# Graph attention edge pass on one core: six buffers of gathered rows, three of the rest, and source lists kept on chip

## The chip, the cores and the metric

The kernel runs on one core of a Trainium2 chip. The metric is the device time of one execution in microseconds (us), lower is better. Engines are named as in the profile: PE is TensorE (PEld its weight loads), DVE is VectorE, ACT is ScalarE, POOL is GpSimd, SP is SyncE.

## What is computed

A graph layer followed by a mixture-of-experts layer. Cut to what the change touches:

```python
N_NODES = 6250                     # x is [6250, 256]; 200,000 edges, sorted by dst; 64 relations
Q = (enh @ Wq + bq).reshape(N, H, D)      # H = 4 heads, D = 64
K = (enh @ Wk + bk).reshape(N, H, D)
V = (enh @ Wv + bv).reshape(N, H, D)
src, dst = (edge_index[0], edge_index[1])
rel = rel_w[edge_relations]
mod_k = K[src] + 0.2 * rel[:, None, :]
scores = jnp.einsum('ehd,ehd->eh', Q[dst], mod_k) / D ** 0.5
seg_max = jax.ops.segment_max(scores, dst, num_segments=N)
ex = jnp.exp(scores - seg_max[dst])
denom = jax.ops.segment_sum(ex, dst, num_segments=N)
w = ex / denom[dst]
agg = jax.ops.segment_sum(w[:, :, None] * V[src], dst, num_segments=N)
```

Then an output projection, a layer norm, a router that picks two of eight experts for each node, the experts, and the combination of their outputs.

## The kernel before, in words

The program is a row of stages, each a block in which every engine has its own instruction stream, and no engine starts a stage before all have ended the last one. `prepare` (L444) makes a table of K and V rows in DRAM (`kv`, 516 float32 values per node), the transposed queries on chip (`QT`), and per-edge features in DRAM. `edge_pass` (L123) does all edges. Then come the node stage, the experts and the combination, which the change leaves alone.

**The edge pass** takes the sorted edges in 261 groups of 768 (`G = 6 * 128`). For one group the work is:

- SP (L186 to L197) loads the group's list of sources (`e_idx`, 128 x 6 integers, L189) and two broadcast rows of features (`e_rows`, L194, L196). Five steps behind, it stores the finished sums (`d_agg`, four DMAs, L207).
- POOL (L215 to L226) issues six gathers (L223), each of which fetches 128 rows of `kv` through one column of `e_idx`. Before them it waits until the sums of the group that last used the buffer are made (`s_agg`, L220) and until the list has landed (L221).
- PE (L354 to L429) turns the K half of the gathered rows (L363, 12 transposes, in two halves of six at two places of a step), multiplies one-hot features (L381) and keys (L386) into scores, adds the weighted V rows (L402, 48 small matmuls per group, which end the use of the gathered rows), and turns the probabilities (L427). A group comes to 12 + 4 + 8 + 2 + 48 + 2 + 4 + 6 = 86 matmuls and as many weight loads.
- DVE empties half of the turned keys (L302), makes `carry` (L312), the one-hot matrix (L317), the maximum (L323) and the sums (L335). ACT fills `e_qblock` from `QT` (L242, L246), empties the other half of the keys (L252), scales the carried sum (L263), takes the exponential (L270) and empties the turned probabilities (L282).

Step g of PE, DVE and ACT works on three groups at once: the key transposes of group g+1, the scores of group g, the sums of group g-1. So PE's step g-1 begins with the rows of group g, and the rows of group g are given back in the middle of step g+1. The order inside a step is written out by hand.

All buffers of the pass exist R = 4 times and the loop is unrolled by R. `pipeline` (L56) writes the first six steps and the last ones out, and puts four steps into the body of a hardware loop. With four buffers, the gathers of group g wait for the sums of group g-4:

```python
                    if g.first >= R:
                        pool.wait_ge(s_agg, g.t - (R - 1))
                    hold(pool, s_idx[g.slot], (g.rnd + 1) * 16)
```

In `prepare` POOL copies the source list from the input into `d_src` in DRAM (L575, L577). Edge e of a group stands at partition e // 6, column e % 6 there, and DVE writes the features of the edges in a matching order with strided reads (L644 to L647).

Of the kernel before, what the change touches and what calls it, by code (L numbers as in the profile page):

```python
# [25 lines left out]
NG = -(-E // G)  # L26
GH = G // 2
# [95 lines left out]
def edge_pass(nc, ctx, cst, QT, kv_dram, src_dram, featx_dram, feat_t_dram, agg_dram, bases, flag, penc, relT):  # L123
# [19 lines left out]
    carry = [sb(f"e_carry{i}", [P, P]) for i in range(R)]  # L143
    acc = [sb(f"e_acc{i}", [P, CW]) for i in range(R)]
    carried = [sb(f"e_carried{i}", [P, CW]) for i in range(R)]
    small = [sb(f"e_small{i}", [P, 8]) for i in range(R)]
# [9 lines left out]
    s_idx = [sem(f"es_idx{i}") for i in range(R)]  # L156
    s_rows = [sem(f"es_rows{i}") for i in range(R)]
    s_kv = [sem(f"es_kv{i}") for i in range(R)]
    s_out = [sem(f"es_out{i}") for i in range(R)]
# [18 lines left out]
    LO, HI, WARM = -1, 2, 6  # L178

    with nc.Block() as blk:  # L180
        @blk.sync
        def _(sp):
            def step(T):
                g = T(0)
                if g.live:

                    if g.first >= R:
                        hold(sp, s_kv[g.slot], g.rnd * (16 * TG))
                    sp.dma_start(idx[g.slot][:, :], src_dram[bass.ds(g.t, 1)].rearrange("a (p t) -> (a p) t", t=TG)  # L189
                                 ).then_inc(s_idx[g.slot], 16)  # L190

                    if g.first >= R:
                        hold(sp, s_oh, g.t - (R - 1))
                    sp.dma_start(rows[g.slot][0:NREL, :],  # L194
                                 feat_t_dram[bass.ds(g.t, 1)].to_broadcast([NREL, G])).then_inc(s_rows[g.slot], 16)
                    sp.dma_start(rows[g.slot][NREL:NR, :],  # L196
# [12 lines left out]
            pipeline(sp, NG, 0, 6, R, WARM, step)  # L209
            for i in range(R):  # L210
                sp.wait_ge(s_out[i], 16 * H * len(range(i, NG, R)))

        @blk.gpsimd
        def _(pool):
            def step(T):  # L215
                g = T(0)
                if g.live:

                    if g.first >= R:
                        pool.wait_ge(s_agg, g.t - (R - 1))  # L220
                    hold(pool, s_idx[g.slot], (g.rnd + 1) * 16)  # L221
# [5 lines left out]
            pipeline(pool, NG, 0, 0, R, WARM, step)  # L227

        @blk.scalar
        def _(act):  # L230
# [3 lines left out]
            def step(T):  # L234
                a = T(-1)
# [51 lines left out]
        def _(dve):  # L287
# [9 lines left out]
            def step(T):  # L297
# [6 lines left out]
                if a.live:  # L304
# [5 lines left out]
                    if a.first >= R:  # L310
                        dve.wait_ge(s_agg, a.t - (R - 1))
# [1358 lines left out]
```

## Time and profile before

| | us |
|---|---|
| Device time, median of 3 runs (4173.77 to 4175.83) | 4174.06 |
| Span of the profiled execution, first to last instruction | 3706.5 |
| What lies around that span, against the median | 467.6 |
| Stage `prepare` | about 0 to 196 |
| Edge pass | about 196 to 2446 |
| Node stage, experts, combination | about 2446 to 3706 |

The profile gives the span of the profiled execution, not its device time, so the third row is the median less the span. Over the span PE is busy 83%, DVE 42%, ACT 35%, POOL 50%, and DMA moves 192 GB/s. "Idle before" in a row is the time that the engine stood still just before those instructions, with what ended it; "issue" means that nothing the profile shows was waited for. A clock of 1.00 is TensorE's full 2.4 GHz, 0.50 is 1.2 GHz.

### The profile page before, as it was taken

The page shows a single profiled execution, that of the slowest core. Times are in us where ns is not written, and L with a number is a line of the kernel's source. Part 1 is how long each engine was busy: PE and PEld are TensorE (multiplying, and loading weights), DVE is VectorE, ACT ScalarE, POOL GpSimd, SP SyncE. Part 2 cuts the span into 40 slices and gives each one's busy share as a digit, 9 for nine tenths or more (in the row PEclk, how much of TensorE's full clock was granted, in tenths as well). Part 3 has the DMA queues.
Part 4 walks back from the last instruction along what each step waited for, and adds up shares of the span by engine and source line. Part 5 has one row for each costly group of instructions (what it writes and reads, how often), then busy time and mean ns, then how long its engine had stood idle before and what let it go on. Part 6 is the DMA issues. An engine that isn't in the chain of part 4 may idle for free. (4 is left out here: it accounts for less than half of the span.)

```text
span 3706.5 us, 94365 instructions
## 1 busy us (share of the span) xinstructions
PE 3077.7 (83%) x27466; PEld 2203.1 (59%) x27466; DVE 1568.6 (42%) x4831; ACT 1314.4 (35%) x3767; POOL 1844.9 (50%) x1996
## 2 busy tenths in 40 slices
PE   6968888888888888888888888867749999999940
PEld 3645555555555555555555555544538888888840
DVE  7734444444444444444444444469941111111123
ACT  1234444444444444444444444423322222222210
POOL 3256777766666666766676666636640000000036
PEclk9978999998899998988899898875559999999975
DMA  7567777777777777776787677744445555555534
GB/s 239 174 185 203 219 222 222 222 211 202 202 209 208 209 204 202 221 200 192 197 222 203 194 214 201 204 126 141 146 162 177 193 175 192 173 195 176 192 101 143
DMA packets 420214, 710.74 MB, mean 192 GB/s; under 512 B 132319, under 2 KB 289783, under 8 KB 420006
## 3 DMA queue, kind: packets, MB, share of 16 engines
q0 software_dynamic: 137328, 450.71, 42.4%
q1 hardware_dynamic: 282822, 259.35, 22.3%
q14 instruction: 46, 0.38, 0.0%
q8 instruction: 18, 0.29, 0.0%
HBM read 637.81 MB, written 72.79 MB: 192 GB/s over the span
## 5 line engine op out<-in xcount | busy, mean ns | idle before, releaser
L223 POOL DMA_INDIRECT e_kv<-d_kv,e_idx x1566 | 1507.7, 963 | 733.7 <-issue 469.8
L363 PE MATMUL psK<-consts,e_kv 128*128 128x128 f32 x3132 | 487.6, 296 | 308.7 <-DMA e_kv<-d_kv,e_idx 308.3
L363 PEld LDWEIGHTS psK<-consts,e_kv 128*128 128x128 f32 x3132 | 363.4, 149 | 379.9 <-issue 345.9
L1577 POOL DMA_INDIRECT c_y<-d_ys,c_idx x98 | 96.4, 984 | 854.6 <-DVE c_idx L1553 825.0
L386 PE MATMUL psD<-e_kT,e_qblock 128*64 128x384 f32 x2088 | 519.4, 581 | 0.0
L302 DVE COPY e_kT<-psK 128x384 f32<-128x384 f32 x522 | 288.5, 553 | 494.3 <-PE psK L363 479.6
L323 DVE TENSOR_REDUCE e_small<-psD 128x1 f32<-128x768 f32 x261 | 249.9, 957 | 512.0 <-PE psD L386 512.0
L1429 ACT ACTIVATE f_hT<-f_psH,f_b 128x256 f32<-128x256 f32 x448 | 212.1, 473 | 590.4 <-PE f_psH L1503 590.4
L263 ACT ACTIVATE e_carried<-psA,e_small 128x65 f32<-128x65 f32 x261 | 82.6, 317 | 922.4 <-PE psA L402 922.4
L1503 PE MATMUL f_psH<-f_xT,f_w 128*128 128x256 f32 x1792 | 398.3, 381 | 1.4 <-DMA f_w<-in_W 1.4
L1493 PE MATMUL f_psY<-f_w,f_hT 128*128 128x256 f32 x1792 | 396.1, 379 | 0.0
L1503 PEld LDWEIGHTS f_psH<-f_xT,f_w 128*128 128x128 f32 x1792 | 342.2, 191 | 48.5 <-DMA f_w<-in_W 1.7
L1493 PEld LDWEIGHTS f_psY<-f_w,f_hT 128*128 128x128 f32 x1792 | 336.3, 190 | 43.3
L252 ACT COPY e_kT<-psK 128x384 f32<-128x384 f32 x522 | 247.8, 475 | 211.6 <-PE psK L363 207.0
L282 ACT COPY e_probT<-psP 128x512 f32<-128x512 f32 (+1 forms) x522 | 224.5, 482 | 71.0 <-PE psP L427 70.4
L381 PE MATMUL psD<-e_onehot,e_qrel_high 98*128 98x384 f32 x522 | 248.3, 476 | 0.0
L402 PE MATMUL psA<-e_kv,e_probT 128*32 128x65 f32 x12528 | 241.9, 228 | 0.3 <-ACT e_probT L282 0.3
L427 PE MATMUL psP<-consts,e_prob 128*128 128x128 f32 x1566 | 228.4, 282 | 12.0 <-ACT e_prob L270 1.9
L270 ACT ACTIVATE e_prob<-psD,e_small 128x768 f32<-128x768 f32 x261 | 234.2, 897 | 5.3 <-DVE e_small L329 5.3
L381 PEld LDWEIGHTS psD<-e_onehot,e_qrel_high 98*128 98x128 f32 x522 | 109.7, 210 | 193.5 <-issue 193.4
L1449 DVE TENSOR_SCALAR f_xT<-f_psT,f_ln 128x256 f32<-128x256 f32 x112 | 55.7, 539 | 398.5 <-PE f_psT L1481 398.5
L402 PEld LDWEIGHTS psA<-e_kv,e_probT 128*32 128x32 f32 x12528 | 198.2, 113 | 19.0 <-ACT e_probT L282 0.5
(202 smaller groups left out, 3766.8 us busy)
## 6 DMA issues: line engine op xcount, KB each, us to landing
f_w<-in_W SPq DMA_DIRECT2D x112, 1024.0 KB, 7.3
e_rows<-d_featt SPq DMA_DIRECT2D x261, 96.0 KB
e_kv<-d_kv,e_idx POOLq DMA_INDIRECT x1566
d_agg<-e_acc SPq DMA_DIRECT2D x1044, 8.1 KB
f_xs<-d_xs SPq DMA_DIRECT2D x56, 256.0 KB, 2.6
d_ys<-f_y SPq DMA_DIRECT2D x56, 256.0 KB, 2.2
e_rows<-d_featx SPq DMA_DIRECT2D x261, 51.0 KB
d_kv<-p_kv SPq DMA_DIRECT2D x48, 258.0 KB, 2.5
```

The lines of the kernel that those rows point to most:

```text
L223: pool.indirect_dma_start(out=kv[g.slot][:, t, :], out_offset=None, in_=kv_dram[:, :], in_offset=bass.IndirectOffsetOnAxis(ap=idx[g.slot][ ...
L252: act.copy(kT[a.slot % 2][:, 1, j * GH:(j + 1) * GH], psK[:, 1, 0:GH]).then_inc(s_kTa, 1)
L270: act.activation(prob[g.slot][:, :].rearrange("p (c q) -> p c q", c=2), psD[:, :, 0:GH], ACT.Exp, bias=small[g.slot][:, NM], scale=SCALE). ...
L302: dve.tensor_copy(kT[a.slot % 2][:, 0, j * GH:(j + 1) * GH], psK[:, 0, 0:GH]).then_inc(s_kTv, 1)
L323: dve.tensor_reduce(sm[:, MX], psD[:, :, 0:GH], AX.XY, ALU.max).then_inc(s_m, 1)
L363: mm = pe.transpose(psK[:, half, t * P:(t + 1) * P], kv[a.slot][:, third * 3 + t, half * P:(half + 1) * P], ident)
L381: pe.matmul(psD[:, c, 0:GH], part[0:NR, :], onehot[g.slot][0:NR, cols], start=k == 0, stop=False)
L386: mm = pe.matmul(psD[half, c, 0:GH], qblock[g.slot][:, b, half], kT[g.slot % 2][:, b, cols], start=False, stop=True, tile_position=(0, hal ...
L402: mm = pe.matmul(psA[h * W:(h + 1) * W, 0:CW], probT[c.slot][:, t, h * W:(h + 1) * W], kv[c.slot][:, t, D + h * CW:D + (h + 1) * CW], star ...
L427: mm = pe.transpose(psP[:, j, (t - lo) * P:(t - lo + 1) * P], prob[g.slot][:, t * P:(t + 1) * P], ident)
L1493: mm = pe.matmul(psY[:, t, 0:D], hT[:, f, t * P:(t + 1) * P], w2[c.slot][:, f, :], start=f == 0, stop=f == FC - 1)
L1503: mm = pe.matmul(psH[:, f % 4, 0:BT], w1[g.slot][:, a, f * P:(f + 1) * P], xT[g.slot][:, a, :], start=a == 0, stop=a == DC - 1)
```

## The change

In the edge pass the unrolling and the buffers of `idx`, `kv`, `carry`, `acc`, `carried` and `small` go from 4 to U = 6, and all others (`rows`, `onehot`, `qblock`, `qrel`, `prob`, `probT`) from 4 to R = 3. The body of the hardware loop holds six steps instead of four, and eight steps stand ahead of it instead of six. The list of sources of a group no longer comes by a DMA from DRAM. All lists stand on chip in `idxall`, and ACT copies six columns of it, five steps ahead of its other work. The gathers of group g wait for the sums of group g-6.

In `prepare` the copy to `d_src` goes. POOL clears a part of `ends` and loads the input's list into it in three DMAs, 128 sources a row. After its other work of the stage, DVE converts the list to float32, PE turns it in 13 transposes of 128 x 128, and DVE writes them back as integers. Edge e of a group now stands at partition e % 128, column e // 128, so the features are written in their own order with plain reads.

```diff
+IT = -(-E // (P * P))
-def edge_pass(nc, ctx, cst, QT, kv_dram, src_dram, featx_dram, ...
+def edge_pass(nc, ctx, cst, QT, kv_dram, idxall, featx_dram, ...
-    R = 4
+    U = 6
+    R = 3
-    idx = [sb(f"e_idx{i}", [P, TG], I32) for i in range(R)]
+    idx = [sb(f"e_idx{i}", [P, TG], I32) for i in range(U)]
-    kv = [sb(f"e_kv{i}", [P, TG, KVW]) for i in range(R)]
+    kv = [sb(f"e_kv{i}", [P, TG, KVW]) for i in range(U)]
...
-    LO, HI, WARM = -1, 2, 6
+    LO, HI, WARM = -1, 2, 8
+    AHEAD = U - 1
...
                     if g.first >= R:
-                        hold(sp, s_kv[g.slot], g.rnd * (16 * TG))
-                    sp.dma_start(idx[g.slot][:, :], src_dram[bass.ds(g.t, 1)].rearrange("a (p t) -> (a p) t", t=TG)
-                                 ).then_inc(s_idx[g.slot], 16)
-
-                    if g.first >= R:
                         hold(sp, s_oh, g.t - (R - 1))
...
-                    if g.first >= R:
-                        pool.wait_ge(s_agg, g.t - (R - 1))
-                    hold(pool, s_idx[g.slot], (g.rnd + 1) * 16)
+                    if g.first >= U:
+                        pool.wait_ge(s_agg, g.t - (U - 1))
+                    hold(pool, s_idx, g.t + 1)
...
             def step(T):
+                n = T(-AHEAD)
+                if n.live:
+
+                    if n.first >= U:
+                        act.wait_ge(s_kv[n.slot], n.rnd * (16 * TG))
+                    act.copy(idx[n.slot][:, :], idxall[:, bass.ds(n.t * TG, TG)]).then_inc(s_idx, 1)
                 a = T(-1)
...
-            pipeline(act, NG, LO, HI, R, WARM, step)
+            pipeline(act, NG, -AHEAD, HI, U, WARM, step)
```

In `prepare`:

```diff
-            pool.dma_start(dram["src"].rearrange("g e -> (g e)")[0:E].rearrange("(a b) -> a b", b=1250),
-                           io["src"].rearrange("(a b) -> a b", b=1250)).then_inc(s_z, 16)
-            pool.dma_start(dram["src"].rearrange("g e -> (g e)")[E:NSRC].rearrange("(a b) -> a b", a=1),
-                           zero[0:1, 0:NSRC - E].bitcast(I32)).then_inc(s_z, 16)
+            pool.memset(ends[:, IT - 1, :], 0).then_inc(s_zero, 1)
+            pool.wait_ge(s_zero, 4)
+            pool.dma_start(ends[:, 0:IT - 1, :], io["src"][0:(IT - 1) * P * P].rearrange("(c r p) -> r c p", p=P, r=P)
+                           ).then_inc(s_src, 16)
...
-                link(dve.tensor_scalar(feat[c][0][0:n, :].rearrange("g (t p) -> g t p", t=TG),
-                                       epos2[0:n, :].rearrange("g (p t) -> g t p", t=TG), -1.0, None, ALU.max))
-                link(dve.tensor_copy(feat[c][1][0:n, :].rearrange("g (t p) -> g t p", t=TG),
-                                     edge[c][1][0:n, :].rearrange("g (p t) -> g t p", t=TG)))
+                link(dve.tensor_scalar(feat[c][0][0:n, :], epos2[0:n, :], -1.0, None, ALU.max))
+                link(dve.tensor_copy(feat[c][1][0:n, :], edge[c][1][0:n, :]))
...
+            dve.wait_ge(s_src, 48)
+            dve.tensor_copy(endsf[:, :, :], ends[:, :, :]).then_inc(s_back, 1)
+            for i, c in enumerate(range(0, IT, 4)):
+                n = min(IT - c, 4)
+                dve.wait_ge(s_turn, i + 1)
+                dve.tensor_copy(idxall[:, c * P:(c + n) * P], psI[:, i % 2, 0:n * P]).then_inc(s_back, 1)
...
+            pe.wait_ge(s_back, 1)
+            for i, c in enumerate(range(0, IT, 4)):
+                if i >= 2:
+                    pe.wait_ge(s_back, i)
+                for j in range(min(IT - c, 4)):
+                    mm = pe.transpose(psI[:, i % 2, j * P:(j + 1) * P], endsf[:, c + j, :], ident)
+                mm.then_inc(s_turn, 1)
```

## Rows read from the trace of the kernel before

**Rows 1.** Waits of the whole span: engine, line, releaser: us in total, times, longest.

```profile
ACT e_carried L263 <- PE psA L402: 922.4, 261, 6.2
...
PE psK L363 <- DMA e_kv<-d_kv,e_idx: 308.3, 187, 21.0
POOL e_kv L223 <- PE psA L402: 246.5, 108, 4.8
```

**Rows 2.** The gathers' line: times, duration ns min/median/max, first and last start.

```profile
L223 POOL DMA_INDIRECT e_kv<-d_kv,e_idx x1566: 940/946/1353, 199.1 to 2422.1; - x196
```

**Rows 3.** Groups by line: busy us, mean ns | idle before and its releasers.

```profile
L223 POOL DMA_INDIRECT e_kv<-d_kv,e_idx x1566 | 1507.7, 963 | 733.7 <-issue 469.8 <-PE psA L402 246.5 <-DMA e_idx<-d_src 17.3
```

**Rows 4.** Timeline of the first groups: start, duration, instruction, [idle before <-releaser].

```profile
206.69 0.95 POOL L223 DMA_INDIRECT e_kv<-d_kv,e_idx  x1 [0.30 <-issue]
207.94 0.95 POOL L223 DMA_INDIRECT e_kv<-d_kv,e_idx  x1 [0.30 <-issue]
...
227.03 0.82 PE L363 MATMUL psK<-consts,e_kv 128*128 128x128 f32 x6
...
233.67 0.82 PE L363 MATMUL psK<-consts,e_kv 128*128 128x128 f32 x6
```

**Rows 5.** Timeline of the regular stretch, one round of the buffers' chain.

```profile
433.96 0.89 PE L402 MATMUL psA<-e_kv,e_probT 128*32 128x65 f32 x48
...
434.98 0.32 ACT L263 ACTIVATE e_carried<-psA,e_small 128x65 f32<-128x65 f32 x1 [3.29 <-PE psA L402]
...
435.74 0.95 POOL L223 DMA_INDIRECT e_kv<-d_kv,e_idx  x1 [0.79 <-issue]
...
438.29 0.87 PE L363 MATMUL psK<-consts,e_kv 128*128 128x128 f32 x6 [1.12 <-DMA e_kv<-d_kv,e_idx]
...
441.94 0.89 PE L402 MATMUL psA<-e_kv,e_probT 128*32 128x65 f32 x48
441.99 0.94 POOL L223 DMA_INDIRECT e_kv<-d_kv,e_idx  x1 [0.30 <-issue]
...
446.04 0.87 PE L363 MATMUL psK<-consts,e_kv 128*128 128x128 f32 x6 [0.90 <-DMA e_kv<-d_kv,e_idx]
```

**Rows 6.** Timeline of the irregular stretches: a late gather, and a step at half clock.

```profile
2408.37 0.94 POOL L223 DMA_INDIRECT e_kv<-d_kv,e_idx  x1 [2.13 <-PE psA L402]
```

```profile
783.35 1.46 PE L363 MATMUL psK<-consts,e_kv 128*128 128x128 f32 x6 [1.63 <-DMA e_kv<-d_kv,e_idx]
...
791.60 0.82 PE L363 MATMUL psK<-consts,e_kv 128*128 128x128 f32 x6
```

**Rows 7.** Windows: us, PE, PEld, DVE, ACT, POOL busy (count), clock, DMA share, GB/s.

```profile
400.00:600.00 200.00, 172.32 (x2151) 114.50 (x2150) 96.47 (x275) 92.19 (x275) 146.34 (x151) 1.00 0.79 221
...
1000.00:1500.00 500.00, 433.07 (x4992) 285.72 (x4993) 225.98 (x638) 216.14 (x642) 335.38 (x350) 0.91 0.74 206
```

```profile
2115.00:2140.00 25.00, 20.84 (x262) 13.96 (x260) 11.93 (x35) 11.38 (x34) 17.85 (x19) 1.00 0.82 233
```

**Rows 8.** Timeline: a gather that starts inside DVE's one-hot instruction.

```profile
447.28 0.61 DVE L317 TENSOR_SCALAR e_onehot<-e_rows,consts 98x768 fp32r<-98x768 bf16 x1
447.41 1.30 POOL L223 DMA_INDIRECT e_kv<-d_kv,e_idx  x1 [0.30 <-issue]
```

**Rows 9.** Timeline of DVE at the start of the program.

```profile
13.95 0.89 DVE L644 TENSOR_SCALAR p_place<-p_epos 128x768 bf16<-128x768 f32 x1
...
15.74 0.56 DVE L637 CAST p_epos<-p_dst 128x768 f32<-128x768 int32 x1
...
42.58 0.43 DVE L674 BATCH_NORM_STATS2 p_stat<-p_x 128x6 f32<-128x256 f32 x1 [3.01 <-DMA p_x<-in_x]
```

**Rows 10.** Timeline of the change from `prepare` to the edge pass.

```profile
188.68 0.41 DVE L707 TENSOR_TENSOR p_q<-p_psQ,p_bias 128x256 f32<-128x256 f32 x1
...
189.16 0.25 SPq L544 DMA_DIRECT2D d_kv<-p_kv  x1
...
196.67 0.27 DVE L289 MEMSET e_qblock<- 128x256 f32 x1 [7.58 <-PEq L513]
...
199.60 0.22 ACT L242 COPY e_qblock<-QT 64x32 f32 x1 [1.77 <-DVE e_prob L294]
```

**Rows 11.** Timeline of DVE in the node stage, just after its loop's branch back.

```profile
2629.09 0.42 DVE L1163 TENSOR_TENSOR n_y<-n_psO,n_xn 128x256 f32<-128x256 f32 x1 [3.17 <-issue]
```

**Rows 12.** Windows of one round each: DVE's node loop, and the edge loop.

```profile
2629.00:2668.00 39.00, 27.09 (x88) 18.54 (x88) 34.81 (x160) 12.08 (x42) 26.60 (x35) 0.59 0.46 145
430.30:464.60 34.30, 30.21 (x360) 19.94 (x362) 16.78 (x47) 15.60 (x47) 25.07 (x26) 1.00 0.80 221
```

More of the change, by code:

```diff
@@ L142, in edge_pass @@
     probT = [sb(f"e_probT{i}", [P, TG, P]) for i in range(R)]
[L143 to L146, printed above, removed]
+    carry = [sb(f"e_carry{i}", [P, P]) for i in range(U)]
+    acc = [sb(f"e_acc{i}", [P, CW]) for i in range(U)]
+    carried = [sb(f"e_carried{i}", [P, CW]) for i in range(U)]
+    small = [sb(f"e_small{i}", [P, 8]) for i in range(U)]
     kT = [sb(f"e_kT{i}", [P, DC, G]) for i in range(2)]
@@ L155, in edge_pass @@
     ident = cst("ident")
[L156 to L159, printed above, removed]
+    s_idx = sem("es_idx")
+    s_rows = [sem(f"es_rows{i}") for i in range(U)]
+    s_kv = [sem(f"es_kv{i}") for i in range(U)]
+    s_out = [sem(f"es_out{i}") for i in range(U)]
     s_init = sem("es_init")
@@ L208, in step @@
                                      ).then_inc(s_out[o.slot], 16)
-            pipeline(sp, NG, 0, 6, R, WARM, step)
-            for i in range(R):
-                sp.wait_ge(s_out[i], 16 * H * len(range(i, NG, R)))
+            pipeline(sp, NG, 0, 6, U, WARM, step)
+            for i in range(U):
+                sp.wait_ge(s_out[i], 16 * H * len(range(i, NG, U)))
         @blk.gpsimd
@@ L291, in _ @@
                 dve.tensor_scalar(qrel[i][1][:, :], cst("pen"), 0.0, None, ALU.mult)
-            dve.memset(acc[R - 1][:, :], 0.0).then_inc(s_init, 1)
-            dve.memset(small[R - 1][:, :], 0.0).then_inc(s_init, 1)
+            dve.memset(acc[U - 1][:, :], 0.0).then_inc(s_init, 1)
+            dve.memset(small[U - 1][:, :], 0.0).then_inc(s_init, 1)
             dve.memset(prob[0][:, 0:1], 0.0).then_inc(s_init, 1)
@@ L316, in step @@
                         dve.wait_ge(s_d, a.t - (R - 1))
-                    dve.tensor_scalar(onehot[a.slot][0:NR, :], rows[a.slot][0:NR, :], cst("match")[0:NR, :], None,
+                    dve.tensor_scalar(onehot[a.slot % R][0:NR, :], rows[a.slot % R][0:NR, :], cst("match")[0:NR, :], None,
                                       ALU.is_equal).then_inc(s_oh, 1)
@@ L379, in step @@
                         cols = slice(c * GH, (c + 1) * GH)
-                        for k, part in enumerate(qrel[g.slot]):
-                            pe.matmul(psD[:, c, 0:GH], part[0:NR, :], onehot[g.slot][0:NR, cols],
+                        for k, part in enumerate(qrel[g.slot % R]):
+                            pe.matmul(psD[:, c, 0:GH], part[0:NR, :], onehot[g.slot % R][0:NR, cols],
                                       start=k == 0, stop=False)
@@ L413, in step @@
                     pe.wait_ge(s_carry, a.t + 1)
-                    pe.matmul(psX[:, 0:1], carry[a.slot][:, :], small[(a.slot - 1) % R][:, MM], start=True, stop=True)
+                    pe.matmul(psX[:, 0:1], carry[a.slot][:, :], small[(a.slot - 1) % U][:, MM], start=True, stop=True)
                     pe.wait_ge(s_qb, a.t * 2 + 2)
                     for b in range(DC):
-                        mm = pe.matmul(psX[0:NREL, P:2 * P], relT, qblock[a.slot][:, b, :],
+                        mm = pe.matmul(psX[0:NREL, P:2 * P], relT, qblock[a.slot % R][:, b, :],
                                        start=b == 0, stop=b == DC - 1)
@@ L480, in prepare @@
     place = sb("p_place", [P, G])
+    ends = sb("p_ends", [P, IT, P], I32)
+    endsf = sb("p_endsf", [P, IT, P])
     misfit = sb("p_misfit", [P, 4])
```

58 lines of the change are left out of this document (34 added, 24 removed).

## The prediction

> **What bounds the kernel now.** I read the waits first. They name a ring of two: PE waits 308.3 us for gathered rows, and POOL, which issues the gathers, waits 246.5 us for PE's sums, that is, for a free buffer [rows 1]. Neither engine is full, so I read the gathers' line next. They run from 199.1 to 2422.1 us, with the last one's 0.95 us 2224.0 us for 261 groups, 8.52 us a group [rows 2]. They are busy 1507.7 us of that; 246.5 us is the wait for PE and the rest is issue time [rows 3]. Three periods then decide the case.
>
> POOL alone: where nothing holds it, a gather starts 1.25 us after the one before, 0.95 us of work and 0.30 us between two [rows 4]. The median of 946 ns makes that gap 0.304 us, and the mean of 963 ns makes a mean pitch of 1.267 us [rows 2, 3]. Six of them are 7.60 us a group.
>
> PE alone: at full clock and with its rows there, one step follows the other in 233.67 - 227.03 = 6.64 us [rows 4].
>
> The ring: from the end of the sums at 434.85 to the first gather 0.89 us; that gather to the sixth's end at 442.93, 7.19 us; until PE starts on the rows at 446.04, 3.11 us; and from a step's start at 438.29 to the end of its sums at 442.83, 4.54 us [rows 5]. That is 15.73 us. With four buffers it spans two steps (the rows of group g are needed at step g-1, and the buffer comes free in step g-3), so a step takes at least 7.87 us. The regular stretch shows 8.0 (2151 matmuls at 86 a group are 25.0 groups in 200 us), at clock 1.00. The middle shows 8.61 (4992 matmuls, 58.0 groups in 500 us), at 0.91 [rows 7]. There the ring has no slack: a wait of 1.63 us for rows came with a clock of 0.50, that step took 8.25 us instead of 6.64, its sums came late, and a later gather waited, as the one of 2.13 us did [rows 6].
>
> **The change, part by part.**
>
> *Six buffers of gathered rows.* The ring now spans four steps: 15.73 / 4 = 3.93 us a step. It stops binding, and POOL's own 7.60 us is the largest period left. All 1566 gathers then take 1566 x 1.267 = 1984.1 us, against 2224.0: minus 239.9 us. POOL no longer waits for PE unless PE falls behind by about two groups, 15 us. What is late next is the gather's issue itself: PE will wait 7.60 - 6.64 = 0.96 us a step, less than the 1.12 us that went with clock 1.00 [rows 5, 7]. Should the clock fall at times, a step of 8.25 us [rows 6] among steps of 6.64 still averages under 7.60, and the filled buffers carry it.
>
> *How sure is 1.267?* The part above 946 ns comes from DVE: a gather that began 0.13 us into the one-hot instruction took 1.30 us [rows 8]. How often they meet depends on the phase, which the change moves. None meeting gives 6 x 1.25 = 7.50 us; the worst, one of 1353 ns [rows 2] in each group, gives 7.91. So the gathers take 1957 to 2065 us, the change gives minus 267 to minus 159 us. I take the mean of today, since the phase today wanders over both.
>
> *The list copied by ACT.* It costs one small copy a group, nearest to the 0.22 us of a `qblock` copy [rows 10], and a few register instructions: 0.2 to 0.5 us. It stands ahead of the `qblock` copies, the key copy, and then the wait for the sums; ACT is idle 3.29 us a step at that wait, 922.4 us in all [rows 1, 5]. In a step of 6.64 us the idle time would still be near 2. Cost nothing; without that cover 0.5 x 261 = 130 us. Its wait for rows of group g-1 has long been met when ACT has finished that group's step. POOL needs the list some four groups later, 30 us. A late list would bring back what was removed.
>
> *The list's DMA and SP.* One DMA fewer and one hold fewer a group on SP, and 128 small pieces less for the DMA engines. No one waited for either but once, 17.3 us at the start, where it stood for the whole change of stage [rows 3]. Gain between nothing and a little less load; I take nothing.
>
> *Three buffers for the rest.* `prob`, `probT`, `onehot`, `qrel` and `qblock` of group g-3 are finished before the step in which group g overwrites them; the waits are met by the order of the steps. `rows` of a group is loaded when the one-hot of three groups before is made and after SP has stored the sums of its step, so some two steps, 15 us, before DVE wants it, one step less than now. Nothing, unless that load took 15 us.
>
> *The loop of six steps.* Priced among the rivals.
>
> *The turned lists in `prepare`.* DVE's conversion: 1664 columns at the 0.56 us for 768 [rows 9] are 1.2 us. 13 transposes at half clock, six in 1.46 [rows 6], are 3.2 us. The copies back, at DVE's 0.41 us for 256 columns out of PSUM [rows 10], are 0.82 us for 512, 2.7 us in all for three and a short one. In series 7.1 us, overlapped about 5.5. DVE ended its work at 189.1 and stood still 7.58 us, because the last store of `kv`, issued at 189.16, had not landed [rows 10]. The work fits into that: nothing, at worst 2 us. On POOL the new memset and one more DMA are a microsecond before a wait of many. DVE's plain reads save up to 0.89 - 0.56 = 0.33 us in each of six instructions, 2 us at most, but 8 us later DVE waits 3.01 us for a DMA [rows 9]; I take nothing.
>
> *Start.* POOL's first gather waits for ACT's first copy instead of a DMA. ACT is free when DVE's clearing ends, which loses one buffer of four, and its first work stood at 199.60 behind a load of a register [rows 10]. Within half a microsecond of now.
>
> **Sum.** 4174.06 - 239.9 = 3934.2, and I forecast 3934. The durations come from the profiled execution, whose span is 3706.5 us; its own device time is not given, so I take what lies around the span (467.6 us) as unchanged and start from the median. The measurement can tell about 0.2%, 8 us, from no change.
>
> **The rivals.**
>
> *The transfers don't keep up.* At 7.60 us a group the DMA engines must deliver 221 x 8.0 / 7.60 = 233 GB/s. Against: one window did 233 at a share of 0.82 [rows 7], and the first gathers ran at full pitch. For: no long stretch has shown more than 221. Held at 8.0 us a group, the gathers take 2088 us: 4038.
>
> *The loop no longer stays where instructions are kept; this one ends slower.* In the node stage DVE stands still 3.17 us after its branch back, for nothing the profile shows, in a round of 160 of its instructions [rows 11, 12]. In the edge pass PE ran some 360 matmuls and as many weight loads a round, and no such wait shows [rows 12]; with six steps it is some 1,030. If it no longer stays, PE stands still in each of 42 rounds, and each such wait costs the clock too: 3.17 + 1.61 = 4.8 us. PE has 6 x 0.96 = 5.8 us of slack a round, so one wait is hidden. The forecast's gain is 5.7 us a round, so beyond 11.5 us, at three waits (14.3), the kernel is slower: 42 x (14.3 - 5.8) = 357, 4291. Against: PE's larger rounds have shown no wait where DVE's small one has, so PE has more room.
>
> The Trainium skill (Runtime: NRT & Kernel Launch, Instruction fetch mechanics) gives the store as 32 KiB for most engines and 128 KiB, 2048 instructions, for PE, and says that a taken branch whose target lies outside the current window of two pages of 256 instructions forces a fetch. By the first figure six steps fit and the forecast stands; by the second even the body of before would have stalled each round, and rows 12 speak against that for PE.
>
> *The edit does not do what it says.* A list that comes late, or one of the three-fold buffers that binds, keeps the ring at about its old length: 4174, no change.
>
> **How the numbers follow.** Forecast, POOL's issue binds: 0.80, with its own range of 3907 to 4015. Transfers hold it at 8.0: 0.11. No change: 0.04. Slower by the loop: 0.05. The last three and the ends make up two in ten outside 3900 to 4018. Faster 0.91, same 0.04, slower 0.05.
>
> **What would show it.** Right: the gathers' idle time before them nearly all issue, the wait for `psA` L402 gone; first to last gather 1984 us apart; PE waiting for rows at nearly each of 261 steps, about 1 us each; clock near 1.00 in the pass; windows near 230 GB/s. The step on DVE is right if gathers still average 963 ns. Wrong: POOL waiting for sums or for ACT's copy; PE or DVE idle by issue every sixth group; gathers landing ever later behind their issue.

## The result, and the profile after

| | before, us | after, us |
|---|---|---|
| Median on record | 4174.89 (4173.77 to 4175.83, 4 runs) | 4198.30 (4192.23 to 4201.73, 4 runs) |
| Ratio, 95% interval | | 1.0051 (1.0037 to 1.0065) |
| Span of the profiled execution | 3706.5 | 4194.8 |
| Its device time | not given | 4196.65 |
| Edge pass, first to last work of an engine | 2245.2 | 2713.8 |

The forecast was 3934 in a range of 3900 to 4018; the changed kernel is 0.5% slower than the one before. The third and fourth lines hold the key. Around the span of the changed kernel lie 1.9 us, not 467.6. So the page of before describes an execution of some 3708 us, by this account, and the executions of 4174 us were others, of which no profile was shown.

The experiments show that there are two conditions, which I name by what the kernel **before** takes in the same comparison. In the light one it takes 3676 to 3742 us and the changed kernel 3471: the medians lie 237.5 us apart, and the 95% interval of the ratio makes that 215 to 251, so the forecast gain of 240 us is there. In the heavy one it takes 4174 to 4185 and the changed kernel 4198. The comparison on record is of the heavy kind.

First the waits of the changed kernel on record (engine, line, what was waited for: us in total, times, longest):

```profile
ACT e_kT L256 <- remote: 960.6, 249, 26.1
POOL e_kv L221 <- PE psA L406: 777.2, 255, 16.5
DVE e_small L327 <- remote: 631.6, 229, 17.0
PEld psA L406 <- issue: 489.3, 521, 2.3
PE psA L406 <- issue: 420.4, 485, 2.2
POOL e_kv L221 <- issue: 399.0, 1310, 0.3
```

PE's wait for gathered rows, 308.3 us before [rows 1], is gone (17.1 us in 4194.8, all of it at the start of the pass). That part of the change works. But POOL's wait for PE's sums did not go away, it trebled, from 246.5 us [rows 1] to 777.2. So PE is late, not POOL. And PE stands still 420.4 us inside its own run of 48 small matmuls, for "issue": nothing that the profile shows. Before, no such row stood among the large ones. ACT and DVE wait for "remote", a signal whose sender the trace doesn't name.

The gathers themselves are as fast as ever, and nobody waits for them (the gathers' line: duration min/median/max, first and last start; then what their engine waited for, and who waited for them):

```profile
L221 POOL DMA_INDIRECT e_kv<-d_kv,e_idx x1566: 940/946/1359, 199.0 to 2875.1; - x196
  PE psA L406: 777.2, 255
  issue: 399.0, 1310
  ACT e_idx L238: 17.9, 1
  PE psK L367: 21.8, 2
```

They take 946 ns as before [rows 2], but their last start is at 2875.1 instead of 2422.1. In the middle PE starts on a group's rows 26 us after the group's last gather was issued.

The windows of the pass (window, its length, busy us and count of PE, PEld, DVE, ACT and POOL, clock, DMA share, GB/s):

```profile
400.00:600.00 200.00, 164.77 (x1695) 111.79 (x1696) 75.27 (x216) 76.17 (x233) 110.89 (x117) 0.88 0.64 172
1000.00:1500.00 500.00, 416.04 (x4160) 288.62 (x4158) 186.20 (x531) 188.28 (x582) 279.87 (x292) 0.86 0.63 172
```

A group has 86 matmuls, so 4160 of them are 48.4 groups in 500 us: 10.34 us a group. The same window of before held 4992, 8.61 us a group [rows 7]. Every period below comes from this window in this way, unless it is called a mean. The clock is lower, 0.86 instead of 0.91, and so is the data rate, 172 GB/s instead of 206 to 221. PE does not wait for rows, so nothing here points at the transfers.

What a stall looks like, in order of time (start, length, engine, line, operation, tile, count, and in brackets the idle time before it):

```profile
1012.12 0.87 PE L390 MATMUL psD<-e_kT,e_qblock 128*64 128x384 f32 x4
...
1013.28 0.43 PE L406 MATMUL psA<-e_kv,e_probT 128*32 128x65 f32 x15
1013.69 0.52 SPq L192 DMA_DIRECT2D e_rows<-d_featt  x1
1014.12 0.95 POOL L221 DMA_INDIRECT e_kv<-d_kv,e_idx  x1 [0.30 <-issue]
1015.19 0.72 SPq L194 DMA_DIRECT2D e_rows<-d_featx  x1
1015.21 0.22 PE L406 MATMUL psA<-e_kv,e_probT 128*32 128x65 f32 x1 [1.50 <-issue]
1016.64 0.74 PE L406 MATMUL psA<-e_kv,e_probT 128*32 128x65 f32 x32 [1.21 <-issue]
1016.67 0.48 ACT L256 COPY e_kT<-psK 128x384 f32<-128x384 f32 x1 [4.39 <-remote]
1016.81 0.96 DVE L327 TENSOR_REDUCE e_small<-psD 128x1 f32<-128x768 f32 x1 [3.34 <-remote]
```

PE does 15 small matmuls in 0.43 us, stands still 1.50 us, does one, stands still 1.21 us, and then does the other 32 in 0.74. ACT and DVE, which had been free for 4.39 and 3.34 us, go on at 1016.67 and 1016.81, in the very moment in which PE does. DVE's instruction reads `psD`, whose last matmul had ended at 1012.99, so the signal reached DVE late. POOL goes on issuing meanwhile, at its 0.95 us and 0.30 between.

### The profile page after: what moved, and what is told of

The parts are those of the page before. It is cut to its first block and busy times, and to the rows that moved or that the text cites. A ratio compares the mean times of both kernels' runs of the same rounds, so it can differ in the third digit from the quotient of the medians.

```text
span 4194.8 us, 93348 instructions
## 1 busy us (share of the span) xinstructions
PE 3383.0 (81%) x27479; PEld 2460.7 (59%) x27479; DVE 1560.9 (37%) x4833; ACT 1363.5 (33%) x4028; POOL 1837.5 (44%) x1998
## 5 line engine op out<-in xcount | busy, mean ns | idle before, releaser
L221 POOL DMA_INDIRECT e_kv<-d_kv,e_idx x1566 | 1500.8, 958 | 1194.1 <-PE psA L406 777.2
L406 PE MATMUL psA<-e_kv,e_probT 128*32 128x65 f32 x12528 | 374.0, 227 | 423.4 <-issue 420.4
L406 PEld LDWEIGHTS psA<-e_kv,e_probT 128*32 128x32 f32 x12528 | 260.6, 110 | 510.6 <-issue 489.3
L367 PE MATMUL psK<-consts,e_kv 128*128 128x128 f32 x3132 | 526.1, 313 | 31.9 <-DMA e_kv<-d_kv,e_idx 17.1
L390 PE MATMUL psD<-e_kT,e_qblock 128*64 128x384 f32 x2088 | 472.2, 532 | 0.0
L367 PEld LDWEIGHTS psK<-consts,e_kv 128*128 128x128 f32 x3132 | 424.3, 163 | 59.6 <-issue 36.3
L431 PE MATMUL psP<-consts,e_prob 128*128 128x128 f32 x1566 | 320.9, 361 | 20.5 <-issue 10.6
L431 PEld LDWEIGHTS psP<-consts,e_prob 128*128 128x128 f32 x1566 | 239.8, 185 | 96.8 <-issue 54.5
L421 PE MATMUL psX<-e_qblock,relT 128*64 128x128 f32 x1044 | 242.0, 374 | 0.0
L385 PE MATMUL psD<-e_onehot,e_qrel_high 98*128 98x384 f32 x522 | 237.1, 454 | 5.7 <-DVE e_qrel_high L345 5.7
```

The costliest lines, as they stand in the source:

```text
L221: pool.indirect_dma_start(out=kv[g.slot][:, t, :], out_offset=None, in_=kv_dram[:, :], in_offset=bass.IndirectOffsetOnAxis(ap=idx[g.slot][ ...
L367: mm = pe.transpose(psK[:, half, t * P:(t + 1) * P], kv[a.slot][:, third * 3 + t, half * P:(half + 1) * P], ident)
L385: pe.matmul(psD[:, c, 0:GH], part[0:NR, :], onehot[g.slot % R][0:NR, cols], start=k == 0, stop=False)
L390: mm = pe.matmul(psD[half, c, 0:GH], qblock[g.slot % R][:, b, half], kT[g.slot % 2][:, b, cols], start=False, stop=True, tile_position=(0, ...
L406: mm = pe.matmul(psA[h * W:(h + 1) * W, 0:CW], probT[c.slot % R][:, t, h * W:(h + 1) * W], kv[c.slot][:, t, D + h * CW:D + (h + 1) * CW], ...
L421: mm = pe.matmul(psX[0:NREL, P:2 * P], relT, qblock[a.slot % R][:, b, :], start=b == 0, stop=b == DC - 1)
```

## The experiments

### Does the light condition exist on its own, and what does each half of the change do there?

Kernel before, sent as it is:

> The kernel before itself, unchanged, to see the execution behind its usual time of 4174 us. Theory A (PE is held to about 10.3 us a group by something that fills up, in both kernels): span about 4172, a group every 10.3 us, freezes of 1 to 2 us inside the 48 small matmuls of line 402, POOL waiting for psA for some 750 us. Theory B (the page of before shows its usual execution, and 467 us lie around the span): span about 3706, a group every 8.5 us, freezes absent, and the slower steps of the changed kernel come from the change.

The lists on chip with four buffers, the changed kernel with

```diff
-    U = 6
-    R = 3
+    U = 4
+    R = 4
-    LO, HI, WARM = -1, 2, 8
+    LO, HI, WARM = -1, 2, 6
```

> The changed kernel with four buffers of everything and a loop of four steps, so only the source lists on chip remain of the change. Theory A: PE's period is the same 10.3 us a group as before and after, time within 0.5% of 4174; whatever makes the changed kernel 0.5% slower shows as a difference either to this or to before. Theory B: about the time of before, with the step of 8.5 us back, if the six-step loop or the six buffers brought the freezes; 4198 with a step of 10.3 us if ACT's list copy brought them.

Measured on one chip: before 3724.02 us (3695.05 to 3779.25, 10 runs), against 3726.25 for the runs of before beside it, ratio 1.0018 (0.9971 to 1.0064); lists alone 3614.30 (3611.14 to 3622.67), ratio 0.9702 (0.9630 to 0.9774). Theory A, which had the stalls in every execution, fell: the edge pass takes 2230.1 us and no small matmul stands still. So did the other half of Theory B, the 467 us around the span: the profiled execution took 3695.05 us with a span of 3693.2. Then the changed kernel itself on another chip, and the six buffers without the lists, that is the kernel before with

```diff
-    R = 4
+    U = 6
+    R = 3
-    kv = [sb(f"e_kv{i}", [P, TG, KVW]) for i in range(R)]
+    kv = [sb(f"e_kv{i}", [P, TG, KVW]) for i in range(U)]
...
-    LO, HI, WARM = -1, 2, 6
+    LO, HI, WARM = -1, 2, 8
```

> The changed kernel once more, unchanged, beside the kernel before on one chip, since before ran in 3726 us in the last runs and its own two-buffer ring shows there with no freezes. Theory C (the 10.3 us a group of the recorded result belongs to the chip or the moment, where before would take 4174 too; elsewhere POOL's issue binds as forecast): about 3726 - 240 = 3486 us, a group every 7.6 us, POOL hardly waiting for psA. Theory D (the changed kernel itself brings the freezes, on any chip): about 4198 us and a group every 10.3 us, whatever before takes.

> Six buffers of gathered rows, three of the rest and the loop of six steps, but the source lists still loaded from DRAM by SP and the preparation as before. Theory C: nearly all of the gain is here, within 15 us of the changed kernel, about 3490 us. Theory D with its cause in the loop or the buffers: about 4198 us here as well; with its cause in ACT's list copy (the lists-only kernel took 3614, so it would need both): about 3490 us.

Measured: the changed kernel 3471.11 us (3468.75 to 3472.67, 4 runs), ratio 0.9372 (0.9324 to 0.9420); six buffers alone 3471.38 (3470.24 to 3473.48), ratio 0.9376 (0.9328 to 0.9424); before beside them 3708.64. Theory C held: one and the same program takes 4198 us in the one condition and 3471 in the other. So with six buffers the lists are worth nothing (0.3 us), and the buffers, with the loop of six steps that comes with them, do all of it. The two were not taken apart in the light condition.

The middle window, 1000 to 1500, of before again, of the lists alone and of the changed kernel in the light condition:

```profile
1000.00:1500.00 500.00, 433.82 (x4988) 287.17 (x4987) 224.73 (x639) 215.55 (x638) 333.89 (x349) 0.91 0.75 206
```

```profile
1000.00:1500.00 500.00, 431.30 (x5246) 286.31 (x5246) 235.50 (x671) 230.43 (x733) 357.32 (x367) 0.97 0.78 216
```

```profile
1000.00:1500.00 500.00, 454.51 (x5666) 303.72 (x5664) 255.48 (x724) 250.07 (x786) 379.98 (x395) 0.99 0.82 232
```

8.62, 8.20 and 7.59 us a group; the clock rises from 0.91 to 0.99. And the waits of the changed kernel in the light condition:

```profile
ACT e_carried L267 <- PE psA L406: 798.1, 261, 5.6
POOL e_kv L221 <- issue: 452.1, 1484, 0.3
PEld psK L367 <- issue: 218.6, 197, 17.4
PE psK L367 <- DMA e_kv<-d_kv,e_idx: 177.0, 173, 17.2
```

This is the picture that the forecast drew: POOL is held by its own issue (its wait for sums is 24.7 us), and it is PE that waits for rows, though at 173 of the 261 steps and not at nearly each.

### In the heavy condition: is it POOL, the ring, or PE's small matmuls?

Three changes of the changed kernel, which met the heavy condition (before 4175.90 us, 4175.53 to 4180.07, 7 runs). The sixth gather replaced by a plain DMA of 128 rows on SP:

```diff
+                    if g.first >= U:
+                        hold(sp, s_agg, g.t - (U - 1))
+                    sp.dma_start(kv[g.slot][:, TG - 1, :], kv_dram[0:P, :]).then_inc(s_kx[g.slot], 16)
...
-                    for t in range(TG):
+                    for t in range(TG - 1):
```

> The changed kernel, but the sixth gather of each group is replaced by a plain DMA of 128 rows of the same table on SP (so the values of a sixth of the edges are other rows than the reference's; bytes and rows moved stay the same). Theory I (the issue of the gathers on POOL bounds the changed kernel, at six times 1.26 us = 7.57 us a group): five issues take 6.3 us, PE's own step of 6.64 us is then the longest, the period falls to 6.65 to 6.9 us and the time on a chip where the kernel before takes 3709 falls from 3471 to 3471 - 0.93 x 261 = 3228, up to 3295. Rival II (the transfers bound it, at 233 GB/s): as many bytes in as many rows are moved, so the period stays at 7.57 and the time at 3471. Where the kernel before takes 4174 on this chip: the period stays near 10.3 whatever POOL does, 4198.

The ring shortened to four steps again, all else kept:

```diff
-                        pool.wait_ge(s_agg, g.t - (U - 1))
+                        pool.wait_ge(s_agg, g.t - (U - 3))
```

> The changed kernel with six buffers, six steps in the loop and the lists on chip, but the gathers of group g wait for the sums of group g-4, as with four buffers. Theory I (the ring is what the change removed): the period goes back to 8.1 us, as in the kernel that had the lists alone (8.14, 3614 us), on a chip where the kernel before takes 3709 to 3726. Rival (the larger loop, or the three-fold buffers, is what made it faster, or the unroll matters by itself): it stays at 7.57 and 3471. Where the kernel before takes 4174: 10.3 us a group and 4198 either way, since the ring had long been loose there (buffers filled 25 us early).

Half of the small matmuls left out:

```diff
-                        for t in range(lo, hi):
+                        for t in range(lo, hi, 2):
                             for h in range(H):
                                 mm = pe.matmul(psA[h * W:(h + 1) * W, 0:CW], ...
```

> The changed kernel with only half of the 48 small matmuls of the sums (L406; the odd sixths of a group are left out of the sums, so the output lacks them). Where the kernel before takes 3709 to 3726: Theory I (POOL's issue bounds, PE has 0.93 us a step to spare) says no change, 3471 within 10 us; were PE the bound, 24 x 0.03 to 0.05 us a step less, 3471 - 0.7 to 1.3 x 261 = 3130 to 3290. Where the kernel before takes 4174: if the limit there is the rate at which PE's dense runs of small matmuls and weight loads may go, some 48 of 187 PE instructions a group fewer give 10.3 x 139/187 = 7.6 to 9.0 us a group, 3490 to 3860; if the limit lies outside PE, the period stays near 10.3 and the time near 4198.

Measured: five gathers 3824.99 us (3815.13 to 3825.81), ratio 0.9150 (0.9135 to 0.9166); ring of four 4199.17 (4196.72 to 4203.48), ratio 1.0055; half the sums 4100.84 (4099.96 to 4104.10), ratio 0.9820 (0.9804 to 0.9836). The ring is indeed without effect here, but the kernel with it did not meet the light condition, in which it would have told the buffers from the loop. Halving the small matmuls takes 97 us or 0.37 us a group. PE needs 0.89 us for 48 of them [rows 5], 0.44 for the 24 left out, so the relief is no more than their own work, and their density is where the stalls show and not what they come from. The surprise is the first: my expectation for this condition was "near 10.3 whatever POOL does", and taking one gather of six from POOL, at as many bytes and rows moved, takes 373 us or 1.43 us a group. PE's stalls fall by half with it, and the granted clock goes back to nearly full (the kernel with five gathers, waits and middle window):

```profile
PEld psA L411 <- issue: 236.1, 312, 1.4
PE psA L411 <- issue: 192.0, 275, 1.4
```

```profile
1000.00:1500.00 500.00, 418.75 (x4856) 275.16 (x4857) 211.23 (x620) 224.61 (x682) 268.02 (x284) 0.99 0.71 200
```

The clock is the larger part of this. The windows of the whole pass, of the changed kernel in the heavy condition, of the one with five gathers, and of the changed kernel in the light condition:

```profile
200.00:2910.00 2710.00, 2225.91 (x22446) 1521.31 (x22446) 1006.22 (x2871) 1016.34 (x3123) 1499.83 (x1566) 0.87 0.63 170
```

```profile
200.00:2540.00 2340.00, 1942.37 (x22418) 1280.56 (x22422) 982.59 (x2870) 1029.96 (x3131) 1237.54 (x1305) 0.98 0.71 197
```

```profile
200.00:2200.00 2000.00, 1811.50 (x22391) 1208.63 (x22392) 1016.16 (x2870) 992.00 (x3120) 1504.20 (x1566) 0.98 0.82 231
```

The granted clock has two levels here, 1.00 and 0.50. It stood at 0.50 for 696 us of the changed kernel's pass, in 664 of which PE was busy, and for 88 and 68 us with five gathers. Six transposes take 1.46 us at half clock and 0.82 at full [rows 6]. If all of PE's work shrinks like these, an estimate, the low clock costs 664 x (1 - 0.82 / 1.46) = 291 us or 1.11 us a group in the one and 0.11 in the other. So of the 1.43 us some 1.0 is the clock that came back, and some 0.4 is the gather that was taken away.

### No gathers, half the rows, half the bytes

So I asked what the gathers do to the other engines. No gather in the pass at all, SP fetching 768 rows by one DMA:

```diff
-                    for t in range(TG):
-                        pool.indirect_dma_start(
...
+                    sp.dma_start(kv[g.slot][:, :, :], kv_dram[0:G, :].rearrange("(t p) d -> p t d", t=TG)
+                                 ).then_inc(s_kv[g.slot], 16)
```

> The changed kernel without any gather in the edge pass: SP fetches 768 fixed rows of the same table for each group with one plain DMA of as many bytes in as many rows (so the sums are of other rows than the reference's). Theory S (on a chip where the kernel before takes 4174, what holds PE, SP and ACT up and makes 10.3 us of a group is the gathers that POOL issues): nothing is held up, no stall inside PE's 48 small matmuls, and PE's own step of 6.64 to 6.9 us bounds the pass, 196 + 261 x 6.7 + 1260 = 3210, up to 3290, on either kind of chip. Rival (it is the transfers' rows and bytes, or the density of PE's instructions, whoever issues them): on such a chip the stalls stay, the group takes 9 us or more and the kernel 3830 or more. On a chip where the kernel before takes 3709 both say 3210 to 3290, unless 1.58 MB in 6.64 us (238 GB/s beside the rest) is more than the transfers manage; then 3471.

Gathers of 64 rows, and gathers of 128 rows of half the length (the buffers are cleared once at the start in both, which costs some 20 us):

```diff
-                            out=kv[g.slot][:, t, :], out_offset=None, in_=kv_dram[:, :],
-                            in_offset=bass.IndirectOffsetOnAxis(ap=idx[g.slot][:, t:t + 1], axis=0),
+                            out=kv[g.slot][0:P // 2, t, :], out_offset=None, in_=kv_dram[:, :],
+                            in_offset=bass.IndirectOffsetOnAxis(ap=idx[g.slot][0:P // 2, t:t + 1], axis=0),
```

```diff
-                            out=kv[g.slot][:, t, :], out_offset=None, in_=kv_dram[:, :],
+                            out=kv[g.slot][:, t, 0:KVW // 2], out_offset=None, in_=kv_dram.rearrange("n (a b) -> (n a) b", a=2),
```

> The changed kernel with gathers of 64 rows instead of 128 (as many instructions on POOL, half the rows and half the bytes; the other half of the edges gets zeros). Where the kernel before takes 4174: Theory S1 (the stalls go with the number of rows gathered): from five gathers of 128 in place of six, 1.43 us a group for 128 rows; 384 fewer rows bring the group down to PE's own step, 6.7 to 7.5 us, 3210 to 3420. Theory S2 (they go with the number of gather instructions): 10.3 us a group, 4198. Where the kernel before takes 3709: if POOL's 0.95 us a gather goes with its rows, PE's step of 6.64 bounds, 3230; if it is a fixed price, the group stays at 7.57 us and the kernel at 3471.

> The changed kernel with gathers of 128 rows of half the length (1032 bytes instead of 2064: as many instructions and rows, half the bytes; the rest of each row is zeros, so the output is another). Where the kernel before takes 4174: Theory S1 (rows) and S2 (instructions) say 10.3 us a group and 4198; Theory S3 (bytes moved for gathers) says as much relief as with half the rows, 3210 to 3420. Where the kernel before takes 3709: Theory I (the issue bounds, not the bytes) says 7.5 us a group, 3450 to 3471; were it the bytes, PE's step bounds, 3230.

These three met the light condition (before 3741.92 us; one of its seven runs took 14353.51 us at full clock, and nothing here explains it): no gathers 3217.30 (3215.30 to 3219.97), ratio 0.8615 (0.8567 to 0.8664); 64 rows 3410.29 (3404.89 to 3415.52), ratio 0.9135; half the length 3498.02 (3490.36 to 3501.79), ratio 0.9370. The middle windows of the three, in this order:

```profile
1000.00:1500.00 500.00, 500.00 (x6500) 346.00 (x6504) 291.34 (x826) 289.14 (x900) 0.00 (x0) 1.00 0.82 266
```

```profile
1000.00:1500.00 500.00, 471.32 (x5887) 314.88 (x5876) 266.50 (x757) 261.89 (x827) 374.71 (x412) 1.00 0.52 134
```

```profile
1000.00:1500.00 500.00, 452.95 (x5676) 301.79 (x5673) 261.72 (x726) 251.03 (x789) 379.37 (x397) 1.00 0.51 129
```

Without gathers PE is busy all the time, at 6.62 us a group, and 266 GB/s flow. With half the bytes in as many rows the group takes 7.58 us, as with all the bytes (7.59): bytes don't bound it. With half the rows a gather takes 0.91 us instead of 0.96, so nearly all of it is a fixed price of the instruction, and the group takes 7.30.

The first two were run again until both had met the heavy condition.

> The same kernel as e7 (no gathers on POOL, one plain DMA of 768 rows a group on SP), which took 3217 us where the kernel before takes 3742, sent again in the hope of a chip on which the kernel before takes 4174. There: Theory S (what holds the engines up is the gathers that POOL issues) says 6.65 us a group and 3210 to 3230, no stall in the small matmuls and no slow register instruction on SP; the rival (rows and bytes whoever issues them, or PE's dense runs) says 9 us or more a group, 3830 or more. On a chip of the other kind: 3217 again, which tells nothing new.

> The same kernel as e8 (gathers of 64 rows instead of 128), which took 3410 us where the kernel before takes 3742. On a chip where the kernel before takes 4174: S1 (the hold-up goes with the rows gathered) says the group falls from 10.3 us to 7.3 (POOL's issue of 64 rows, as measured) up to 8.2, 3410 to 3650; S2 (it goes with the number of gather instructions) says 10.3 us a group, 4198. On a chip of the other kind: 3410 again.

> The kernel without gathers on POOL once more, for a chip on which the kernel before takes 4174. There Theory S (the gathers that POOL issues cause the hold-ups) says 3210 to 3230 and no stall in the small matmuls; the rival (rows and bytes whoever issues them, or PE's dense runs) says 3830 or more. On a chip of the other kind: 3217 again.

> The kernel with gathers of 64 rows once more. On a chip where the kernel before takes 4174: S1 (the hold-up goes with the rows gathered) says 3410 to 3650; S2 (with the number of gather instructions) says 4198. On a chip of the other kind: 3412 again.

> The kernel without gathers on POOL once more, for a chip on which the kernel before takes 4174. There Theory S (the gathers that POOL issues cause the hold-ups) says 3210 to 3230 and no stall in the small matmuls; the rival (rows and bytes whoever issues them, or PE's dense runs) says 3830 or more. On a chip of the other kind: 3217 again.

> The kernel with gathers of 64 rows (384 rows a group in six instructions), sent again now that without gathers the kernel took 3239 where the kernel before takes 4182. On such a chip: S1 (the hold-up goes with the rows gathered) says the group falls from 10.3 us to 7.3 up to 8.2, 3410 to 3650; S2 (with the number of gather instructions) says 10.3 us a group, 4198. On a chip of the other kind: 3412 again.

> The kernel with gathers of 128 rows of half the length (1032 bytes). On a chip where the kernel before takes 4174 to 4182: S1 and S2 (rows or instructions) say 10.3 us a group and 4198 to 4220; S3 (the bytes that gathers move) says 7.6 to 8.8 us a group, 3500 to 3800. On a chip of the other kind: 3498 again.

> The kernel with gathers of 64 rows, one last time. On a chip where the kernel before takes 4174 to 4182: S1 (the hold-up goes with the rows gathered) says 3410 to 3650; S2 (with the number of gather instructions) says 4198 or more. On a chip of the other kind: 3410 to 3417 again.

| run | before, us | this, us | ratio (95%) |
|---|---|---|---|
| no gathers, second | 3725.01 | 3215.97 | 0.8673 (0.8627 to 0.8720) |
| 64 rows, second | 3725.01 | 3413.53 | 0.9206 (0.9157 to 0.9254) |
| no gathers, third | 3734.44 | 3218.33 | 0.8621 (0.8534 to 0.8708) |
| 64 rows, third | 3734.44 | 3416.33 | 0.9151 (0.9058 to 0.9244) |
| **no gathers, fourth** | **4182.15** | **3239.01** | 0.7745 (0.7722 to 0.7767) |
| 64 rows, fourth | 3676.36 | 3417.49 | 0.9293 (0.9266 to 0.9320) |
| half the length, second | 3676.36 | 3502.81 | 0.9525 (0.9498 to 0.9553) |
| **64 rows, fifth** | **4185.27** | **4262.87** | 1.0184 (1.0154 to 1.0214) |

The two bold lines decide. Without gathers the kernel takes nearly the same in both conditions, and its window in the heavy one is that of the light one:

```profile
1000.00:1500.00 500.00, 500.00 (x6460) 345.44 (x6458) 290.73 (x826) 289.56 (x901) 0.00 (x0) 1.00 0.81 266
```

Its edge pass takes 1753.9 us there and 1753.2 in the light condition. As many bytes and rows moved by SP, and 48 small matmuls as dense as ever, and no stall: Theory S is shown as it was put, the rival (rows and bytes, or PE's density) fell. SP fetches the same 768 neighbouring rows for every group, however, and through another queue. So whether it is the instruction on POOL, the queue that its packets go through or the scattered rows that holds PE up, this run alone can't tell. Half the rows in as many gathers, on the other hand, bring no relief at all, which speaks against the scattered rows. The waits and the middle window of that kernel in the heavy condition:

```profile
POOL e_kv L224 <- PE psA L412: 881.4, 255, 17.4
PEld psA L412 <- issue: 516.3, 525, 2.2
PE psA L412 <- issue: 446.8, 510, 2.7
```

```profile
1000.00:1500.00 500.00, 415.17 (x4116) 290.60 (x4115) 184.49 (x523) 185.50 (x573) 261.81 (x287) 0.84 0.36 94
```

10.45 us a group at 94 GB/s, against 7.30 us of the same kernel in the light one. S2 held: the stalls (446.8 us instead of 420.4) go with the number of gather instructions, not with their rows. Rows of half the length met the light condition both times, so for those nothing is known of the heavy one. All of these kernels but the ring of four compute other sums, so none is a remedy; one instruction that gathers more rows, which would lower their number, was not tried.

## Why the prediction was wrong

**The step that failed** is in the sum: "its own device time is not given, so I take what lies around the span (467.6 us) as unchanged and start from the median". Nothing of that size lies around a span: 1.9 us do in the changed kernel. The 467.6 us lay inside executions in another condition. Of them 1.9 us belong around the span. If before loses as much in the node stage and the combination as the changed kernel does (3.3 and 14.6 us, last section), 448 us are left for the pass, 1.72 us a group on top of 8.52 [rows 2]: 10.24. The changed kernel's gathers, counted in the same way, take (2875.1 + 0.95 - 199.0) / 261 = 10.26 us a group. (No profile of before in the heavy condition was taken; this is worked out.) So there the longest period was already PE's step with what the gathers cost it, and not the ring that the forecast loosens. In the changed kernel the ring of four is hidden below it (ring of four 4199, ring of six 4198), and loosening it could win nothing. What makes the changed kernel 0.5% slower was not found; it is not the longer ring. The three rivals of the prediction all reasoned from the same page and so missed it too. The one without a change came near in its time, 4174, by luck, for its reason was another: neither did a list come late nor did a buffer of the three-fold ones bind.

The remaining terms can be held against the light condition, for which the page of before is a true picture:

- *The gain.* 3708.64 - 3471.11 = 237.5 us (215 to 251 by the interval), forecast 239.9. The gathers start from 199.0 to 2180.1 us, with the last one's 0.95 us 1982 us, forecast 1984.1.
- *POOL's period.* Mean over the groups from the eighth on 7.60 us, forecast 7.60; a gather's mean is 0.961 us instead of 0.963, so DVE's share stayed as I took it.
- *PE's step.* 6.62 to 6.66 us without gathers, forecast 6.64.
- *The ring.* With the lists alone the mean is 8.17 us, my bound was 7.87; a ring of six has its buffer free 14 us before POOL wants it (median).
- *Transfers as the rival.* Fell: 232 GB/s are held for the whole pass, and 266 without gathers.
- *The larger loop as the rival.* Fell: no stall comes every sixth group in the light condition, and the six-step loop gives 3471 with the lists and without. The page of the changed kernel counts few packets of instructions (queue, kind: packets, MB, share) in the whole program:

```profile
q8 instruction: 19, 0.31, 0.0%
q14 instruction: 48, 0.39, 0.0%
```

  So the Trainium skill's rule (Runtime: NRT & Kernel Launch, Instruction fetch mechanics), by which a taken branch to outside the current window of two pages forces a fetch, cost PE's loop nothing, as rows 12 had it for the smaller loop.
- *The lists on chip.* I took nothing. With six buffers that is right. With four it was wrong: 0.9702, 112 us, the period fell from 8.46 to 8.17 us on average and the clock in the middle rose from 0.91 to 0.97. PE stood at half clock for 299 us of the pass before and for 119 with the lists (285 and 113 of them busy), which by the estimate above is 172 x 0.44 / 261 = 0.29 us a group, the whole fall. The two profiled executions lie 72 us apart, less than the medians. Whether it is the list's DMA, SP's wait for it or the 128 small pieces that lowered the clock was not tried.
- *`prepare`.* Nothing, as forecast: the pass begins at 196.2 us in the changed kernel and at 196.5 before.

The list of what would show the forecast wrong did name "PE or DVE idle by issue", but every sixth group; it came in nearly each group, inside L406.

**What stays open:** by what path a gather instruction holds up PE, SP, ACT and the signals, and what makes the condition. With the low clock taken out as estimated above (780 us of PE's work at half clock, 1.31 us a group, with gathers of 64 rows) a gather costs PE nearly the same in all three: (10.34 - 6.65 - 1.11) / 6 = 0.43 us for each of six, (8.86 - 6.65 - 0.11) / 5 = 0.42 for each of five, and (10.45 - 6.65 - 1.31) / 6 = 0.42 for each of six with 64 rows. Nor is it shown to belong to a chip: in the experiments it was met under three chip numbers (0, 7 and 12), never under 2, 3, 4 and 9, and under number 0 before took 4175.90 at one time and 3676.36 later.

## What to carry to other kernels

Hold the span of a profile against the device time of the runs before reasoning from it: here some 2 us lie between them, and hundreds mean that the page shows a condition in which the runs were not made. A ring that is loosened pays down to the next period and only if that ring is the longest in the condition that is measured; ask of the other engines, too, what they cost there. A short stall of PE can cost more than its length, where the clock falls with it: compare the clock before putting a difference down to the stalls. In a kernel like this one the number of gather instructions counts twice, 1.25 us each on POOL and, in the heavy condition, some 0.4 us each on PE with the low clock on top. Half the rows in as many instructions save 61 us in the light condition and nothing in the heavy one, half the length nothing in the light one.

## What the runs showed of the hardware that I had not expected

- A gather of 64 rows takes 897 ns, one of 128 rows 946, and one of 128 rows of half the length 946 (medians; the first of these kernels, then the last):

```profile
L224 POOL DMA_INDIRECT e_kv<-d_kv,e_idx x1566: 890/897/1300, 218.2 to 2121.5; - x196
```

```profile
L224 POOL DMA_INDIRECT e_kv<-d_kv,e_idx x1566: 942/946/1314, 219.3 to 2203.4; - x196
```

- In the heavy condition the engines that suffer in the pass are PE, ACT and SP. PE's stops inside the small matmuls are mostly about 0.5 or 1.2 us long. SP's register instructions, 29 to 42 ns in the median, took about 0.7 us more than 300 times, ACT's some tens of times; in the light condition, loads of registers aside, none took over 0.2. Of the register arithmetic of DVE and POOL none was slow in either.
- The other stages say the same. From the first to the last work of an engine the experts, with no gather, take 810 to 811 us in both conditions. The combination, with 98 gathers, takes 132.3 us in the changed kernel in the light condition and 146.9 in the heavy one, the node stage 302.0 and 305.3. Without gathers in the edge pass the combination still does so, 132.3 and 149.8, which shows that this kernel, too, ran in the heavy condition. There DVE waits for issue (the groups of one line of the combination, heavy condition, then light, in the kernel without gathers in the edge pass: busy, mean ns, idle before, what ended it):

```profile
L1590 DVE SCALAR_TENSOR_TENSOR c_two<-c_y,c_wb,c_one 128x256 f32<-128x256 f32 x49 | 24.0, 489 | 27.3 <-issue 11.6 <-DMA out<-c_two 7.3 <-DVE c_one L1584 3.9
```

```profile
L1590 DVE SCALAR_TENSOR_TENSOR c_two<-c_y,c_wb,c_one 128x256 f32<-128x256 f32 x49 | 23.8, 486 | 8.4 <-DVE c_one L1584 6.3
```
